# First steps of a four-layer attention kernel: table load ahead, zero matmuls ahead, first queries into a score bank, first keys by head from PSUM

## The reference

```python
qkv = tgt @ sa_in_w.T + sa_in_b
q, k, v = jnp.split(qkv, 3, axis=-1)
q, k, v = (heads(q, T), heads(k, T), heads(v, T))
scores = jnp.einsum('bhtd,bhsd->bhts', q, k) * SCALE
attn = jax.nn.softmax(scores, axis=-1)
```

## Time and profile before

| | us |
|---|---|
| three runs | 224.49, 227.08, 230.85 |
| median | 227.08 |
| profiled execution, its own time | 224.79 |
| span of the profiled execution | 222.2 |
| around the span | 2.6 |

### The profile page before, as it was taken

The page is one execution under the profiler, slowest core; times in us unless marked ns, Lnnn a source line. Parts: engine busy times, 40 slices in busy tenths (PEclk is TensorE's granted clock), DMA queues, the critical chain, the costliest instruction groups (busy, mean ns, idle before and its releaser), DMA issues.

```text
span 222.2 us, 11019 instructions
## 1 busy us (share of the span) xinstructions
PE 193.2 (87%) x4951; PEld 147.3 (66%) x4951; DVE 128.7 (58%) x227; ACT 119.9 (54%) x308; POOL 36.0 (16%) x61
## 2 busy tenths in 40 slices
PE   2798789999999999989798878899997799899935
PEld 0376568767886787668565656667686648588834
DVE  0599999996745227942378744442835226555950
ACT  1254740674756777477625652744769436763802
POOL 2990300131120131112011000111010003100000
PEclk9999996999999999999999999999999769999999
DMA  5990000000000000000000000000000000000002
GB/s 140 372 379 20 0 6 4 6 4 3 6 3 3 0 3 0 3 3 3 4 6 3 3 6 3 3 6 3 3 3 3 6 3 1 3 3 3 6 27 71
DMA packets 3901, 6.25 MB, mean 28 GB/s; under 512 B 528, under 2 KB 3216, under 8 KB 3600
## 3 DMA queue, kind: packets, MB, share of 16 engines
q1 hardware_dynamic: 3856, 5.57, 7.4%
HBM read 5.04 MB, written 0.52 MB: 25 GB/s over the span
## 4 chain that ended last, share of the span: by engine, by line
PE 67%; issue 9%; ACT 6%; DVE 5%; POOLq 1%; POOL 1%; DVEq 0%; ACTq 0%
PE bank L453 31%; PE score L456 20%; PE bank L697 12%; PE bank L669 4%; ACT probs_sb L801 2%; DVE probs_sb L1042 2%; ACT att_sb L845 1%; DVE m_col_sb L963 1%; POOLq L323 1%; DVE v_ext_sb L936 1%; DVE att_sb L1027 1%; ACT L801 1%; DVE v_ext_sb L933 1%; ACT xa_sb L850 0%; ACT probs_sb L799 0%
## 5 line engine op out<-in xcount | busy, mean ns | idle before, releaser
L963 DVE TENSOR_REDUCE m_col_sb<-score 128x32 f32<-128x2048 f32 (+1 forms) x16 | 30.2, 1889 | 11.8 <-PE score L456 11.6
L453 PE MATMUL bank<-v_ext_sb,probs_sb 128*32 128x18 f32 (+1 forms) x2176 | 28.5, 193 | 8.1 <-issue 6.4
L453 PEld LDWEIGHTS bank<-v_ext_sb,probs_sb 128*32 128x32 f32 x2176 | 24.7, 115 | 15.3 <-issue 13.5
L801 ACT ACTIVATE probs_sb<-score 128x1024 f32<-128x1024 f32 (+1 forms) x28 | 26.2, 962 | 13.0 <-PE score L456 12.9
L1082 POOL TENSOR_SCALAR vare_sb<-var_sb 128x2 f32<-128x2 f32 x20 | 5.2, 261 | 140.7 <-ACT att_sb L845 140.7
L453 PE MATMUL bank<-xa_sb,W_sb 128*128 128x256 f32 x64 | 21.3, 448 | 6.9 <-DMA W_sb<-in_mats 3.3
L905 DVE TENSOR_TENSOR k_heads_sb<-k_kept_sb,small_sb 128x1024 f32<-128x1024 f32 x12 | 14.7, 1226 | 16.5 <-ACT k_kept_sb L820 16.4
L914 DVE TENSOR_TENSOR q_heads_sb<-q_kept_sb,small_sb 128x1024 f32<-128x1024 f32 x16 | 19.5, 1222 | 6.5 <-ACT q_kept_sb L810 3.8
L845 ACT ACTIVATE att_sb<-bank 128x128 f32<-128x128 f32 x40 | 10.7, 274 | 21.5 <-PE bank L697 21.4
L456 PE MATMUL score<-k_heads_sb,q_kept_sb 32*64 32x256 f32 x384 | 18.0, 413 | 3.0 <-issue 2.2
L456 PE MATMUL score<-q_heads_sb,k_kept_sb 32*64 32x256 f32 x512 | 20.1, 400 | 0.4 <-issue 0.4
(11 more groups left out here) (120 smaller groups left out, 360.6 us busy)
## 6 DMA issues: line engine op xcount, KB each, us to landing
W_sb<-in_mats SPq DMA_DIRECT2D x1, 1152.0 KB, 7.6
W_sb<-in_mats SPq DMA_DIRECT2D x1, 1024.0 KB, 9.8
ctxT_sb<-in_ctxT SPq DMA_DIRECT2D x1, 512.0 KB, 5.1
cn_sb<-in_ctx SPq DMA_DIRECT2D x1, 512.0 KB, 11.3
hid_sb<-in_idx SPq DMA_DIRECT2D x1, 512.0 KB, 7.3
out<-attT_sb SPq DMA_DIRECT2D x4, 128.0 KB, 1.8
xa_sb<-in_xT SPq DMA_DIRECT2D x1, 384.0 KB, 3.9
W_sb<-in_mats SPq DMA_DIRECT2D x1, 192.0 KB, 2.8
```

The costliest lines, as they stand in the source:

```text
L453: return pe.matmul(o, l, r, start=start, stop=stop)
L801: act.activation(dst, src, ACT.Exp, scale=SCALE).then_inc(sem("exp"), 1)
L963: dve.tensor_reduce(o, src, AX.X, ALU.max).then_inc(sem("max"), 1)
```

## The change

Four edits; the order of the steps on every engine stays as it was.

1. ACT runs an exponential of a small constant tile as its first instruction, after POOL's `half` is written.
2. DVE first writes zeros into a new tile `warm` (128x512, bf16). PE, once that is done, runs 6 matmuls of 512 columns on it into `bank[3]` before its first step, and 4 more between q0 and s0.
3. q0 is written into the first bank of `score` instead of `bank[0]`, and no longer waits for the bank; `q_kept` of group 0 reads it there.
4. For all four groups of `sa`, `k_heads` is made from the projection in PSUM by one `scalar_tensor_tensor` (add bias, multiply by mask) instead of from `k_kept`. `k_kept` of `sa` now waits for `k_heads` of its group.

```diff
+WARM = (6, 4)
...
+            def busy(n):
+                for _ in range(n):
+                    mm(bank[G - 1][:, :], warm[:, 0:128], warm[:, :])
...
+            pe.wait_ge(sem("warm_ready"), 1)
+            busy(WARM[0])
             for step, name, g, i in ORDER:
+                if step == "s" and name == "sa" and g == 0:
+                    busy(WARM[1])
...
-                    o = take("q", name, g)
+                    if name == "sa" and g == 0:
+                        o = score[:, 0, :]
+                    else:
+                        o = take("q", name, g)
...
+            act.wait_ge(sem("half_ready"), 1)
+            act.activation(warm_act[:], half[:], ACT.Exp)
             act.wait_ge(sem("v_loaded"), 16)
...
                 if step == "q_kept":
                     act.wait_ge(sem("q"), nth("q", name, g))
+                    src = (score[:, 0, :] if name == "sa" and g == 0 else bank[g])[:, 0:GT]
...
                 elif step == "k_kept":
                     act.wait_ge(sem("k"), nth("k", name, g))
+                    if name == "sa":
+                        act.wait_ge(sem("k_heads"), nth("k_heads", name, g))
...
+            dve.memset(warm[:], 0.0).then_inc(sem("warm_ready"), 1)
...
+                if name == "sa":
+                    dve.wait_ge(sem("k"), nth("k", name, g))
+                    dve.wait_ge(sem("v_loaded"), 16)
+                    dve.scalar_tensor_tensor(k_heads[HEADS[name]][:, g, :, :],
+                                             bank[g][:, 0:GT].unsqueeze(1).to_broadcast([128, HH, GT]), col("sa_kb"),
+                                             const("head").unsqueeze(2).to_broadcast([128, HH, GT]), ALU.add, ALU.mult
+                                             ).then_inc(sem("k_heads"), 1)
+                    return
```

More of the change, by code:

```diff
@@ L369, in build @@
         half = sb("half", [128, 8])
+        warm = sb("warm", [128, 512], BF)
+        warm_act = sb("warm_act", [128, 8])
         WC = sb("WC", [128, 9, 128])
@@ L707, in hidden @@
                 last.then_inc(sem("h"), 1)
+            def busy(n):
+                for _ in range(n):
+                    mm(bank[G - 1][:, :], warm[:, 0:128], warm[:, :])
+            first = [k for k in ORDER if k[0] in ("k", "q", "s")][:3]
+            assert first == [("k", "sa", 0, 0), ("q", "sa", 0, 0), ("s", "sa", 0, 0)], first
+            pe.wait_ge(sem("warm_ready"), 1)
+            busy(WARM[0])
             for step, name, g, i in ORDER:
+                if step == "s" and name == "sa" and g == 0:
+                    busy(WARM[1])
                 if step == "weights":
@@ L806, in _ @@
                     act.wait_ge(sem("q"), nth("q", name, g))
+                    src = (score[:, 0, :] if name == "sa" and g == 0 else bank[g])[:, 0:GT]
                     if name == "l3":
-                        last = act.activation(q_kept[:, g, :], bank[g][:, 0:GT], ACT.Copy)
+                        last = act.activation(q_kept[:, g, :], src, ACT.Copy)
                     else:
-                        last = act.activation(q_kept[:, g, :], bank[g][:, 0:GT], ACT.Identity,
-                                              bias=col(f"{name}_qb"), scale=1.0)
+                        last = act.activation(q_kept[:, g, :], src, ACT.Identity, bias=col(f"{name}_qb"), scale=1.0)
                     last.then_inc(sem("q_kept"), 1)
```

## The result

The changed kernel takes 233.81 us in the median of four runs (231.95 to 235.61), the kernel before 225.79 in the median of four (224.29 to 230.85). The ratio is 1.032, 95% interval 1.024 to 1.040: **slower, by 3.2%**. The forecast was 226.5 with a range of 223.5 to 230.0.

A forecast was written before the change was run, and what follows sets the result against it. It took DVE's gapless stream up to 28 us, then PE, as the bound, with max1's start as gauge: 224.79 + 0.45 + 0.15, called +0.5, 225.3; by the median 227.6; middle 226.5, range 223.5 to 230.0.

The forecast's parts named there:

- The table load: On ACT at the start: loading moves to about 0.85 to 2.2 us, removing 1.28 us in front of k_kept0.
- PE's wait ahead of q1: Group 1 on PE: idle some 2.5 us, from k2's end at about 10.0 us until q1 at 12.5.
- the head start is spent in group 1: From max0's end to max1's start takes 6.9 us instead of 4.45, using up the 2.0 us gained at max0.
- The new operation: k_heads from PSUM on DVE: 1.23 us for 1024 elements, with 0 to 0.1 us more for the source.
- Six wide zeros: On PE before k0: 2.4 us at half clock (1.9 to 3.7), leaving PE free at 3.5 us.
- rival (a): PE's clock falls again in the stand before q1, slowing q1, k3, q3, s1: +2.5 us, 227.7 or 230.0; chance 0.22.
- The first step that failed: Zeros cost about 0.2 us ahead of k0 (0 to 1.4); the other four hide in the wait for q_kept0.
- the step that opens the argument: After 28 us PE's waits are short, so work reaching it later or sooner shifts the end by about as much.
- the term of +0.45 us for max1: max1 on DVE starts at 17.6 us instead of 17.16, behind k_kept1's wait for k_heads1, with s1 at full clock.
- its terms of 0.45 and 0.15: 0.45 us for max1's later start, 0.15 us for the ends of the new operation; stated together as +0.5.
- The last sentence of the prediction: Prediction is wrong if max1 starts clearly before 17.2 us, or low-clock stretches after 28 us differ in number or length.
- 0.10 of the chances: Chance of a result more than 2% (4.5 us) slower, from the clock falling again with run spread on top.

The follow-up runs named there:

- g4_after_again: The changed kernel run once more, unchanged, beside other variants: 235.29 us against 229.92 for the kernel before.
- e2_no_zeros: The changed kernel without the zeros (no memset, wait or extra matmuls), other three edits kept: 231.36 us, ratio 1.017 to the kernel before.
- g1_after_pad54: The changed kernel plus 54 zero matmuls of 8 columns in PE's wait ahead of q1: 228.31 us, ratio 1.007 to the kernel before.
- g3_after_thin: The changed kernel with its ten zero matmuls cut from 512 to 8 columns: 234.50 us, ratio 1.033 to the kernel before.
- f4_after_pad118: The changed kernel plus 118 zero matmuls of 8 columns ahead of its own ten: 232.83 us, ratio 1.036 to the kernel before.
- f1_pad128: The kernel before plus 128 zero matmuls of 8 columns ahead of its first step: 231.22 us, ratio 1.015 to the kernel before.
- f2_pad64: The kernel before plus 64 zero matmuls of 8 columns ahead of its first step: 228.65 us, ratio 1.021 to the kernel before.
- h96_group0: The changed kernel with keys by head from PSUM for group 0 alone and 90 narrow zeros replacing the four wide ones: 221.00 us against 228.49 before.
- i3_h96_again: Rerun of h96_group0, unchanged: 221.04 us, ratio 0.977 to the kernel before.
- g2_after_pad118: The changed kernel plus 118 zero matmuls of 8 columns in PE's wait ahead of q1: 231.01 us, ratio 1.021 to the kernel before.

## Why the prediction was wrong

**The start was right.** The table load, s0 at 1.12 us, k_kept1 released by k_heads1, PE's wait ahead of q1 (2.5 us predicted, 2.79 measured) and max0 (8.40 predicted, 8.39 measured) came as worked out. So did the finding that the head start is spent in group 1: 2.03 us ahead at max0, behind at max1. The new operation took 1.28 us instead of 1.23, inside the 0 to 0.1 allowed. Six wide zeros took 2.74 us against 2.4. k0 and q0 still ran at half clock; it rose while the first of the four others ran, and these took 1.07 us against the 0.9 predicted at the full clock.

**max1 was 18.54 instead of 17.6**, because rival (a) happened in this execution: the clock is at 0.58 from 12 to 14 us and q1, k3 and q2 take 2.90 us. It cost 0.9 us, not the 2.5 that (a) priced, since it was over before q3 and s1. In the profile of g4_after_again the clock stays up there, the same three take 1.86 us, and max1 starts at 17.62, the forecast's number:

```profile
12.60 1.86 PE L456 MATMUL bank<-xa_sb,W_sb 128*128 128x256 f32 x6 [2.79 <-ACT k_kept_sb L841]
```

So the number 17.6 holds only for the clock that it assumed. In whole, with s1 at 2.01 us, (a) happened in the profiles of e2_no_zeros, g1_after_pad54 and g3_after_thin, which have the same waits of k_kept for k_heads; their max1 starts at 19.77, 19.06 and 20.54. Such a wait doesn't lower the clock each time: in g4_after_again one of 2.79 us, in f4_after_pad118 one of 2.80 us left it up.

**The first step that failed** is the one on the zeros: "So the zeros cost about 0.2 us ahead of k0 (0 to 1.4)", with the wait for q_kept0 as their cover. I priced their time on the array and what hid it, not their place in PE's instruction stream. Their price was paid from 107 us on: alone, as narrow ones, ten records have a ratio of 1.016, about 3.5 us. With it fell the step that opens the argument, that after 28 us work "that reaches PE later at 28 us ends later by about the same amount": this takes the waits behind it as fixed. I had read the waits on issue, 12.4 us of them, as short and as a sign that PE is the bound, and didn't ask what they were or that their place depends on the number of instructions ahead. In sum they were the largest wait in the kernel; the next was the 3.3 us for the first matrix.

**The second step that failed** is the term of +0.45 us for max1, which rests on a clock that is up by s0 and stays up. It isn't the zeros that make the rest of the loss: without them the other three edits have a ratio of 1.017 (1.006 to 1.027), 3.8 us, where the prediction had 0.5 us for the whole change (its terms of 0.45 and 0.15 make 0.6, a slip that decides nothing). In that profile max1 is 2.6 us later, some 1.4 of it by the low clock. With the new wait in group 0 alone and no zeros the ratio is 1.004, so this loss belongs to k_kept waiting for k_heads in groups 1 to 3, which the prediction had found, and to the clock, which it had put among the rivals at 0.22. The 1.2 to 1.6 us beyond max1 are within what four runs leave open.

The sizes: of the 9.2 us of span, 1.4 are max1. The waits on issue give 2.6 (15.0 less 12.4). The profile has 17.6 us more at half clock, of which 3.4 are at 12 us and already counted in max1; the other 14.2 are worth at most 7.1 if PE is the bound throughout. 1.4 + 2.6 + 7.1 is 11.1, above the 9.2, as it must be when PE isn't always the bound. By runs rather than profiles the direction is the same: the mean low-clock time is 28.0 us against 17.0 of the kernel before. The account is rough, though: take max1, the waits on issue and half the low-clock time from the medians of the table, and what is left runs from 185.3 us (g3_after_thin) to 191.6 (f1_pad128) instead of being one number.

The last sentence of the prediction named the sign ("if the low-clock stretches after 28 us differ in number or length"), but gave it no mechanism on the slower side and 0.10 of the chances.

**Open.** That the low clock follows the waits on issue is read from where it falls in the traces, and from the two kernels that differ in narrow zeros alone (26 and 15 us); no run holds the waits fixed and alters the clock. Nor do the waits alone order the kernels: f2_pad64 has 15.3 us of them and only 13.8 us of low clock. Why 96 records do better than none, and 64 better than 10, was not predicted; it was found. h96_group0 and i3_h96_again gain with as much low clock as before (17.2 and 17.6 us): there it is the waits (9.3 and 7.9 us against 12.3) and the earlier max1. Whether ten wide zeros cost more than ten narrow ones is open too: 3.8 us on the kernel before, 0.8 on the changed one. And f1_pad128 with borders as before is 3.0 us above before in the medians, 2.0 more than its later start, within what six runs leave open.

## What to carry to other kernels

In a kernel of thousands of very short matmuls, count the instructions that an edit adds or removes ahead of such a stretch, not only their time: block borders of the code move, and here ten useless matmuls alone cost 3.0 us (narrow) or 6.8 (wide) in the medians, and 96 useless ones gained 5.7. Idle time of PE with no releaser is worth a look of its own: that these waits lay multiples of 256 instructions apart was the sign that they were for code. Before believing or rejecting an edit of that kind, run it at two or three paddings. And when an order is strict on each engine, a new wait (here k_kept for k_heads) must be followed through everything queued behind it in the next group, not only in the one for which it was made.

## What the runs showed of the hardware

- PE's waits on issue over 0.25 us lie 256 PE instructions or a multiple apart (all 218 intervals in twenty profiles, to within two; 124 to 127 matmul records for one block), end 1.07 to 1.64 us after a 16 KB packet of the code queue has landed (all 238), and where two of them stand one block apart they are never closer than 3.3 us. They return to the same matmuls when 128 records are added (37 and 27 of 64 in the kernel before, in e2_no_zeros, g2_after_pad118 and f4_after_pad118; 27 and 37 with ten added).
- A narrow zero matmul of 8 columns takes 27 ns in a row (54 in 1.49 us), so 96 of them fit in a wait of 2.8 us.
- In the changed kernel the six wide zeros and the two records each of k0 and q0 start 0.43 us apart, the last three of the four zeros behind q0 0.22 us apart: TensorE's clock rose from 1.2 to 2.4 GHz at about 5.5 us, where before s0 still ran at the lower one at 8.30 us. It fell again at 12 us in one profile and not in another of the same kernel, after the same wait of 2.79 us, nor in f4_after_pad118 after 2.80. In e2_no_zeros, g1_after_pad54 and g3_after_thin it was at half from about 14 to 21 us, behind waits of 1.82, 1.46 and 2.08 us, so the length of the last wait doesn't tell when it falls.
